# Routing each token tile inside the self-attention loop, with overflow blocks numbered as tiles open them

## The chip, the cores and the metric

The kernel runs on one core of one Trainium2 chip. The metric is the device time of one execution in microseconds (us). Three executions gave 1191.19 to 1192.11, with a median of 1192.05.

The core's engines run side by side: TensorE (PE, matrix products and transposes), VectorE (DVE), ScalarE (ACT), GpSimd (POOL) and SyncE (SP, which starts most transfers). Each works through its own list of instructions in order and waits for the others by semaphores.

## The reference

The program is a small network of two layers on `x` of 16 sequences x 64 tokens x 256 features: six residual sub-blocks, each behind a layer norm. What matters here is the third, the sub-block `L0_ffn`: an attention and then a mixture of 8 experts, of which each token uses two.

```python
h = _layernorm(x, ln1_g, ln1_b)
x = x + attention(h, Wq, Wk, Wv) @ Wo            # 16 heads of 16, within each sequence
m = _layernorm(x, ln2_g, ln2_b)
probs = jax.nn.softmax(m @ Wg, axis=-1)          # 8 experts
wts, idx = jax.lax.top_k(probs, 2)
wts = wts / jnp.sum(wts, axis=-1, keepdims=True)
h1 = jax.nn.gelu(einsum('td,edf->etf', m, W1) + b1[:, None, :])     # F = 1024
ye = einsum('etf,efd->etd', h1, W2) + b2[:, None, :]
moe_out = sum over the two chosen experts of wts * ye
return x + moe_out
```

Before it stands `L0_attn` (a latent attention with rotary parts, "mla" in the code), after it a cross attention, a causal attention ("attn") and a dense feed-forward part.

## The kernel before

The 1024 tokens are 8 tiles (`T`) of 128 rows; `x[:, t, :]` stays on chip. The stages run one after the other on every engine's list: `*_x0` (first cross attention), `*_self(span 0)`, `*_moe`, `*_x1`, `*_self(span 1)`, `*_ff`.

`*_self(span 0)` handles 16 items, the list `ITEMS`: mla of tiles 0, 1, 2, then in turn ffn (the attention of `L0_ffn`) of tile t-3 and mla of tile t, and at the end the ffn attention of tiles 5, 6, 7. So items 3, 5, 7, 9, 11, 13, 14, 15 are "ffn". The loop is software pipelined by hand: iteration n does the front of item n (transposed input `hT`, `q`/`k`/`v` or `rope`/`lat`/`qkc`, then the `scores`) and the back of item n-1 (`neg`, `exponents`, `pv`, `T`, `y`). The order on each engine is that of the calls in `pe_self`, `act_self`, `dve_self`, `pool_self`. Everything that TensorE hands over goes through four PSUM banks used in turn: the list `SA_FILLS` is the order of the fills, and `Ring.wait_free` makes a fill wait until the fill four places earlier has been read. The scores use four other banks.

On VectorE iteration n has: `k` or `rotate`, (`residual(n-2)` where item n is mla), `norm(n+1)`, `attend(n-1)`, `maximum(n)` (three instructions: a reduction of 128x1024 and two small ones that make `neg`), then `residual(n-1)`, which also starts the statistics of the next norm. GpSimd turns statistics into a factor (`row_rstd`) and adds `u` to `x` (`add_u`).

`*_moe` begins when the last item is finished. All 8 tiles are normed (`row_apply` "moe", 8 instructions, L372), transposed by TensorE (L1761) and scaled by ScalarE (`mT`, L1847), multiplied with `Wg` (`router`, L1752). VectorE takes the two largest of 8 (L1921, L1923), makes `pick` (which expert is first, which second choice) and `picked`. TensorE turns `picked` into ranks by matmuls with a triangle `before` and with `ones` (L1769 to L1774). Rows of expert e go to slots 256e to 256e+255 of the DRAM array `moe_in`; rows of rank 256 and more go to overflow blocks behind the eight first ones (NB = 15 blocks of 256 rows in all, the loop always computes all 15). VectorE works out the slots (L1939 to L1964), GpSimd then scatters each tile's rows twice, by an indirect transfer each (L2066, 16 in all). SP waits for the 16, loads blocks of `moe_in` (`xg<-moe_in`), and TensorE starts on block 0: `rows_T(0)` (L1794), `hidden(0)` (L1809).

Beside this stand: `gate`, the weights of the two experts per token, which TensorE transposes (L1779) and multiplies with `b2` (L1784) before `rows_T(0)` in its list; VectorE adds the result to `x` (L2008) before its part of `rows_T(0)` (L2015, L2017). Expert weights are split into a high and a low part: `expert_upper` on ScalarE, `expert_lower` on VectorE (L1737), `expert_lower_pool` on GpSimd (L1742).

## Time and profile before

| | |
|---|---|
| median of 3 runs | 1192.05 us |
| the profiled execution: its time, its span | 1194.0 us, 1192.0 us |
| busy in the span: PE, DVE, ACT, POOL | 1048.1, 617.5, 476.6, 240.5 us |
| `*_self(span 0)`: first `hT` to the last `residual` | 376.0 to 562.95 us |
| from there to `hidden(0)` | 562.95 to 615.94 us |

The profile was taken of one execution; its span runs from the first instruction to the last. "Idle before" in a row is the time in which the engine had nothing to do before this instruction, with what released it. PEclk is the share of TensorE's full clock (2.4 GHz) that was granted in a stretch: 0.50 is the lower of its two levels, 1.2 GHz, all the time.

### The profile page before, as it was taken

To read this page: it belongs to the slowest core of one execution; us is meant where nothing else is said; L and a number is where in the kernel's file an instruction comes from. 1 tells how busy PE (TensorE), PEld (TensorE's weight loads), DVE (VectorE), ACT (ScalarE), POOL (GpSimd) and SP (SyncE) were. 2 spreads that over 40 slices of the span, in tenths; PEclk is the share of its full clock that TensorE was granted. 3 is DMA by queue.
4 is the path that set the end of the run, shared out by engine and by line. 5 is a ranking of instruction groups with operands and counts; after the bars stand their busy time and mean duration, and the time that the engine had idled before them with its cause. 6 is when DMAs were issued, how large, how long until landed. Compare 5 with 4: busy or idle time off the path is not lost.

```text
span 1192.0 us, 27308 instructions
## 1 busy us (share of the span) xinstructions
PE 1048.1 (88%) x11708; PEld 902.8 (76%) x11708; DVE 617.5 (52%) x1205; ACT 476.6 (40%) x868; POOL 240.5 (20%) x381
## 2 busy tenths in 40 slices
PE   3999999999996899997539999986999988997998
PEld 3778888888875777775539999975878766775787
DVE  3745445454223444443628999965565632344342
ACT  1423333332322544553326677742434331443332
POOL 2211211211111121212343444423201000010000
PEclk9999999999998798997579999997999986997999
DMA  9200000000003400000065666622110002000000
GB/s 306 73 19 19 15 5 19 1 1 1 1 1 129 182 2 2 2 2 2 23 206 180 235 206 230 221 72 79 37 38 19 2 2 63 2 2 1 1 18 18
DMA packets 55670, 72.77 MB, mean 61 GB/s; under 512 B 8504, under 2 KB 48896, under 8 KB 54912
## 3 DMA queue, kind: packets, MB, share of 16 engines
q1 hardware_dynamic: 54016, 66.85, 16.8%
q0 software_dynamic: 1536, 4.20, 1.1%
...
q14 instruction: 25, 0.20, 0.1%
...
## 4 chain that ended last, share of the span: by engine, by line
PE 73%; DVE 12%; ACT 6%; issue 4%; POOL 3%; DMA 1%; DVEq 0%; SPq 0%; ACTq 0%; POOLq 0%
PE ps L1809 6%; PE ps L1827 6%; PE ps L527 5%; PE ps L2141 5%; PE ps L512 5%; PE ps L1384 4%; PE ps L991 3%; PE ps L1312 3%; PE ps L545 3%; PE ps L565 3%; PE ps L466 3%; PE ps L496 2%; PE ps L1346 2%; PE ps L928 2%; ACT sa_pT L1500 2%
## 5 line engine op out<-in xcount | busy, mean ns | idle before, releaser
L350 POOL TENSOR_TENSOR rn_tmp<-rn_cur,eps 128x1 f32<-128x1 f32 x48 | 13.4, 280 | 505.0 <-DVE rn_cur L344 505.0
L641 ACT ACTIVATE x0pT<-ps 128x512 f32<-128x512 f32 x64 | 38.3, 598 | 120.6 <-PE ps L527 120.6
L1809 PE MATMUL ps<-moe_xT_hi,ew_1hi 128*128 128x256 f32 x240 | 69.0, 287 | 2.3 <-DVE moe_xT_lo L2017 2.3
L1827 PE MATMUL ps<-ew_2hi,eh_hi 128*128 128x256 f32 x240 | 69.3, 289 | 1.1 <-DVE eh_lo L2025 1.1
L1809 PE MATMUL ps<-moe_xT_lo,ew_1hi 128*128 128x256 f32 x240 | 68.5, 286 | 0.0
L1809 PE MATMUL ps<-moe_xT_hi,ew_1lo 128*128 128x256 f32 x240 | 68.4, 285 | 0.0
L1827 PE MATMUL ps<-ew_2hi,eh_lo 128*128 128x256 f32 x240 | 67.4, 281 | 0.0
L1827 PE MATMUL ps<-ew_2lo,eh_hi 128*128 128x256 f32 x240 | 67.4, 281 | 0.0
L2023 DVE CAST eh_hi<-eh 128x512 fp32r<-128x512 f32 x60 | 58.8, 980 | 13.1 <-ACT eh L1878 13.0
L2025 DVE TENSOR_TENSOR eh_lo<-eh,eh_hi 128x512 fp32r<-128x512 f32 x60 | 60.2, 1003 | 2.1
L805 POOL TENSOR_SCALAR x0pT<-x0pT 128x512 f32<-128x512 f32 x64 | 39.3, 614 | 105.2 <-ACT x0pT L641 103.4
L1384 PEld LDWEIGHTS ps<-sa_v,sa_pT 64*64 64x64 f32 x1536 | 48.5, 139 | 15.3 <-ACT sa_pT L1500 15.3
L2141 PE MATMUL ps<-f,ffw 128*128 128x512 f32 x256 | 59.3, 391 | 0.3 <-DVE f L2212 0.3
L730 DVE COPY x0v<-ps 128x512 f32<-128x512 f32 x32 | 22.1, 691 | 68.9 <-PE ps L512 68.9
L1384 PE MATMUL ps<-sa_v,sa_pT 64*64 64x18 f32 x1536 | 50.9, 211 | 6.1 <-ACT sa_pT L1500 3.5
L2141 PEld LDWEIGHTS ps<-f,ffw 128*128 128x128 f32 x256 | 47.7, 188 | 10.9 <-DVE f L2212 1.1
L512 PE MATMUL ps<-x0wv_hi,x0cT_hi 128*128 128x512 f32 x128 | 53.3, 416 | 0.0
L724 DVE TENSOR_TENSOR x0A_lo<-ps,x0A_hi 128x512 fp32r<-128x512 f32 x64 | 40.5, 684 | 23.1 <-ACT x0A_hi L632 23.1
L527 PE MATMUL ps<-x0A_hi,x0cT_hi 128*128 128x512 f32 x128 | 51.3, 401 | 0.0
L512 PE MATMUL ps<-x0wv_hi,x0cT_lo 128*128 128x512 f32 x128 | 50.8, 397 | 0.0
L1742 POOL TENSOR_TENSOR ew_1lo<-ew,ew_1hi 128x1024 fp32r<-128x1024 f32 x15 | 39.1, 2608 | 57.5 <-ACT ew_1hi L1732 57.5
L512 PE MATMUL ps<-x0wv_lo,x0cT_hi 128*128 128x512 f32 x128 | 50.7, 396 | 0.0
...
## 6 DMA issues: line engine op xcount, KB each, us to landing
...
```

Of the source, the lines that this page charges most:

```text
L512: last = nc.tensor.matmul(dst, m[:, k, tok * P:tok * P + P], w[:, k, half * 512:half * 512 + 512], start=(k == 0 and n == 0), stop=(k == K ...
L527: last = nc.tensor.matmul(ps[:, S_BANK[u % 2], :], w[:, k, keys], m[:, k, b, pg, :, :, :].rearrange("p a j n -> p (a j n)"), start=(k == 0 ...
L641: nc.scalar.activation(g.pT[:, u, :], ps[:, S_BANK[u % 2], :], ACT.Exp, scale=64.0 ** -0.5).then_inc(C0.exp, 1)
L724: nc.vector.tensor_tensor(g.A_lo[:, kc, :, pg, par, :, :].rearrange("p b j n -> p j b n"), bank_of(t, f"A{gr}{par}").rearrange("p (j b n) ...
L805: nc.gpsimd.tensor_scalar(g.pT[:, u, :], g.pT[:, u, :], high, low, ALU.min, ALU.max).then_inc(C0.clip, 1)
L1384: last = nc.tensor.matmul(RS.bank(n, "pv")[rows_b, hd * XVW:hd * XVW + XVW], g.pT[rows_b, r, at_p:at_p + N], g.v[n % 2][rows_b, hd, :], st ...
L1742: nc.gpsimd.tensor_tensor(lo, w, hi.bitcast(F32), ALU.subtract).then_inc(MO.w_lo_pool, 1)
L1809: last = nc.tensor.matmul(ps[:, n % 3, j * BT:j * BT + BT], w[b % 2][:, i, f * P:f * P + P], v[b % 2][:, i, :], start=(i == 0 and m == 0), ...
L1827: last = nc.tensor.matmul(ps[:, O_BANK[b % 2] + c, 0:D], v[n % 3][:, j * BT + c * P:j * BT + c * P + P], w[b % 2][:, f, :], start=(f == 0 ...
L2023: nc.vector.tensor_copy(eh_hi[n % 3][:, :], eh[n % 3][:, :]).then_inc(MO.hi, 1)
L2025: nc.vector.tensor_tensor(eh_lo[n % 3][:, :], eh[n % 3][:, :], eh_hi[n % 3][:, :].bitcast(F32), ALU.subtract).then_inc(MO.split, 1)
L2141: last = nc.tensor.matmul(ps[:, 2 + f % 4, :], w[:, k, f * P:f * P + P], src[part][:, k, :], start=(k == 0 and part == 0), stop=(k == ks - ...
```

## The change

The work of the routing moves from `*_moe` into `*_self(span 0)`, one tile at a time:

- Behind the last fill of iteration n, where item n-2 is ffn (and item n is not mla), TensorE transposes the normed tile (`fill_mT(n-2)`). VectorE norms that tile (`moe_norm(n-2)`) behind `maximum(n)`. ScalarE scales it (`mT`).
- An iteration later, where item n-3 is ffn, TensorE does `fill_router(n-3)` and `fill_rank(n-3)`, VectorE `route_top`, `route_rank` and `route_slot`, GpSimd the two scatters of the tile. These three kinds of fills are new entries of `SA_FILLS`, so they take banks of the ring.
- Five tiles are routed inside the loop (at n = 6, 8, 10, 12, 14). Those of items 13, 14 and 15 are routed in a written-out end behind the loop, in which the back of item 15 stands too.
- A tile's slots must be known before later tiles are counted. So an expert's rows 256 and up no longer go to blocks numbered by expert, but to the next free block when a tile makes the count pass the end of the current one. `block_end`, `block_off`, `next_block`, `end_slot` carry this from tile to tile; the owner of each overflow block is found at the end from `opened`.
- The splits of expert 0 move one iteration forward on ScalarE and VectorE, and from `pool_moe` into iterations 14 and 15 on GpSimd.

```diff
         SA_FILLS = []
         for _lo, _hi in SPANS:
...
                 if is_mla(_n):
-                    SA_FILLS += [(_n, "rope")] + [(_n - 1, "neg")] * (_n > _lo) + [(_n, "lat")] + [(_n - 2, "y")] * late_y(_n - 2)
-                    SA_FILLS += [(_n - 1, "pv")] * (_n > _lo) + [(_n, "qkc"), (_n, "v")] + [(_n - 1, "T")] * (_n > _lo) + [(_n + 1, "hT")]
+                    SA_FILLS += [(_n, "rope")] + [(_n - 1, "neg")] * _bk + [(_n, "lat")] + [(_n - 3, "router")] * _rt + [(_n - 2, "y")] * late_y(_n - 2)
+                    SA_FILLS += [(_n - 1, "pv")] * _bk + [(_n, "qkc"), (_n, "v")] + [(_n - 1, "T")] * _bk + [(_n - 3, "rank")] * _rt + [(_n + 1, "hT")]
...
         def pe_self(pe, span):
...
+            if span == 0:
+                fill_neg(hi - 1)
+                fill_router(hi - 3)
+                exponents(hi - 1)
+                fill_mT(hi - 2)
+                fill_pv(hi - 1)
+                fill_rank(hi - 3)
+                fill_router(hi - 2)
+                fill_T(hi - 1)
+                fill_y(hi - 1)
+                fill_rank(hi - 2)
+                fill_mT(hi - 1)
+                fill_router(hi - 1)
+                fill_rank(hi - 1)
...
         def dve_self(dve, span):
...
+            def moe_norm(n):
+                t = ITEMS[n][1]
+                dve.wait_ge(SA.x_done, t + 1)
+                row_apply(dve, t, u[:, t, :], [u[:, t, :]], "moe")
...
+                route = span == 0 and is_ffn(n - 3)
                 if is_mla(n):
                     rotate(n)
                 elif front:
                     k(n)
+                if is_mla(n) and route:
+                    route_top(dve, n - 3)
                 if late_y(n - 2):
                     residual(n - 2)
...
                 if is_mla(n):
                     v(n)
+                    if route:
+                        route_rank(dve, n - 3)
                 if front:
                     maximum(n)
+                if route and not is_mla(n):
+                    route_rank(dve, n - 3)
+                if span == 0 and is_ffn(n - 2):
+                    moe_norm(n - 2)
+                if route:
+                    route_slot(dve, n - 3)
                 if back and not late_y(n - 1):
                     residual(n - 1)
-                if span == 0 and n > hi - 2:
-                    expert_lower(dve, 0, 2 * (n - hi + 1))
+                if span == 0 and n >= hi - 2:
+                    expert_lower(dve, 0, 2 * (n - hi + 2))
...
+            if span == 0:
+                route_top(dve, hi - 3)
+                moe_norm(hi - 2)
+                attend(hi - 1)
+                route_rank(dve, hi - 3)
+                route_slot(dve, hi - 3)
+                route_top(dve, hi - 2)
+                residual(hi - 1)
+                route_rank(dve, hi - 2)
+                moe_norm(hi - 1)
+                route_slot(dve, hi - 2)
+                route_top(dve, hi - 1)
+                route_rank(dve, hi - 1)
+                route_slot(dve, hi - 1)
...
         def pool_self(pool, span):
...
+                if span == 0 and is_ffn(n - 3):
+                    scatter(n - 3)
+                if span == 0 and n in (hi - 2, hi - 1):
+                    expert_lower_pool(pool, 0, 2 * (n - hi + 2) + 1)
...
+        def route_slot(dve, n):
+            t = ITEMS[n][1]
+            dve.wait_ge(MO.route, ROUTE[t, "opens"])
+            nc.vector.tensor_tensor(oless[:, :, :], less[:, :, :], each(opens[:, t:t + 1, :], (E, E)), ALU.mult).then_inc(MO.route, 1)
...
+            nc.vector.tensor_copy(slot[:, 2 * t:2 * t + 2], slotf[:, t, :]).then_inc(MO.slot, 1)
...
+            nc.vector.tensor_tensor(opened[:, t, :], block_id[:, :], opens[:, t, :], ALU.mult).then_inc(MO.route, 1)
...
+            nc.vector.tensor_tensor(end_slot[:, :], block_off[:, :], block_end[:, :], ALU.add).then_inc(MO.route, 1)
```

**Place 1: TensorE, from iteration 5 into iteration 6.** L1392/L1416 are the transposes `T`, L1281/L1305 `hT`, L1295/L1319 `rope`, L1353/L1377 `neg`, L1400/L1424 `y` (line of before / of the change). Before:

```order
L1392 MATMUL ps<-cst,sa_att 128x128 x2
L1281 MATMUL ps<-cst,h 128x128 x2
L1295 MATMUL ps<-sa_hT,w_mla 128x128 x8
L1353 MATMUL ps<-identb,sa_neg 128x128
L1287 MATMUL ps<-sa_hT,w_mla 128x128 x2
```

The change, the same place:

```order
L1416 MATMUL ps<-cst,sa_att 128x128 x2
L1305 MATMUL ps<-cst,h 128x128 x2
L1431 MATMUL ps<-cst,u 128x128 x2
L1319 MATMUL ps<-sa_hT,w_mla 128x128 x8
L1377 MATMUL ps<-identb,sa_neg 128x128
L1311 MATMUL ps<-sa_hT,w_mla 128x128 x2
```

The two transposes of the normed tile (L1431, `fill_mT`) now stand between `hT` and `rope`.

**Place 2: VectorE, from the end of iteration 6 into iteration 7.** L1578/L1668 is the last of `maximum`, L1596/L1686 with `u` the start of `residual(5)`, L1568/L1658 the copy `k(7)`. Before:

```order
L1578 SCALAR_TENSOR_TENSOR sa_neg<-sa_max,sa_neg 128x4x4
L1596 TENSOR_TENSOR u<-ps,u 128x256
L341 BN_STATS rn_st<-u 128x6
L344 BN_AGGR rn_cur<-rn_st 128x2
L1568 COPY sa_kT_133<-ps 128x256
```

The change, the last of the 16 instructions of `route_slot(3)` and what follows:

```order
L1927 TENSOR_TENSOR block_off<-block_off,moved_n 128x8
L1928 SCALAR_TENSOR_TENSOR block_end<-opens,block_end 128x8
L1930 TENSOR_SCALAR next_block<-next_block,opens_n 128x8
L1932 TENSOR_TENSOR end_slot<-block_off,block_end 128x8
L1686 TENSOR_TENSOR u<-ps,u 128x256
L359 BN_STATS rn_st<-u 128x6
L362 BN_AGGR rn_cur<-rn_st 128x2
L1658 COPY sa_kT_147<-ps 128x256
```

All 16 stand between `maximum(6)` and `residual(5)`, and so ahead of `k(7)`.

**Place 3: TensorE, the end of span 0.** Before, behind `scores(15)`:

```order
L1392 MATMUL ps<-cst,sa_att 128x128 x2
L1400 MATMUL ps<-w_sq_65,sa_attT 128x256 x2
L1353 MATMUL ps<-identb,sa_neg 128x128
L1366 MATMUL ps<-sa_negT,pick_neg 128x128 x4
L1370 MATMUL ps<-sa_qbd_131,sa_kT_133 64x128 x8
```

The change, from the same transposes `T(14)` to `pv(15)` (L1408):

```order
L1416 MATMUL ps<-cst,sa_att 128x128 x2
L1431 MATMUL ps<-cst,u 128x128 x2
L1424 MATMUL ps<-w_sq_65,sa_attT 128x256 x2
L1377 MATMUL ps<-identb,sa_neg 128x128
L1438 MATMUL ps<-wg,sa_mT 128x8 x2
L1390 MATMUL ps<-sa_negT,pick_neg 128x128 x4
L1394 MATMUL ps<-sa_qbd_145,sa_kT_147 64x128 x8
L1390 MATMUL ps<-sa_negT,pick_neg 128x128 x4
L1394 MATMUL ps<-sa_qbd_145,sa_kT_147 64x128 x8
L1431 MATMUL ps<-cst,u 128x128 x2
L1408 MATMUL ps<-sa_v_149,sa_pT 64x18 x32
```

`mT(13)`, `router(13)` and `mT(14)` have come in ahead of `y(14)`, of the exponents of item 15 and of its `pv`.

## Rows read from the trace of the kernel before

**Rows 1.** The page: busy time of each engine and share of the span

```profile
PE 1048.1 (88%) x11708; PEld 902.8 (76%) x11708; DVE 617.5 (52%) x1205; ACT 476.6 (40%) x868; POOL 240.5 (20%) x381
```

**Rows 2.** Windows (stretch, busy us per engine, PEclk, DMA share, GB/s), the scatter

```profile
583.00:612.00 29.00, 8.29 (x40) 6.50 (x40) 11.38 (x41) 4.33 (x6) 19.77 (x18) 0.62 0.25 84
```

**Rows 3.** Windows, two pairs of iterations, cut where `rope` starts on PE

```profile
446.09:469.32 23.23, 21.84 (x344) 18.12 (x344) 9.81 (x28) 10.64 (x23) 4.71 (x14) 0.87 0.01 3
...
491.40:512.08 20.68, 19.29 (x345) 15.93 (x345) 9.82 (x28) 10.64 (x23) 4.71 (x14) 1.00 0.01 2
```

**Rows 4.** Chain that ended last (start us, us, what), from the last residual on

```profile
562.95 0.43 DVE u L1596
...
586.58 0.18 DVE slot L1964
...
587.63 1.22 POOL moe_in L2066
...
607.32 2.40 DMA moe_in<-u,slot
...
614.73 0.44 DVE moe_xT_hi L2015
...
615.94 4.13 PE ps L1809 x21
```

**Rows 5.** Timeline around a `rope` (start us, us, engine, line, operation, idle before)

```profile
491.40 2.05 PE L1295 MATMUL ps<-sa_hT,w_mla 128*128 128x128 f32 x16 [0.77 <-ACT sa_hT L1462]
491.58 0.17 DVE L1578 SCALAR_TENSOR_TENSOR sa_neg<-sa_max,sa_neg 128x16 bf16<-128x16 f32 x1
```

**Rows 6.** Timeline of an ffn iteration: `residual`, `v`, `add_u`, `pv`

```profile
482.86 0.42 DVE L1596 TENSOR_TENSOR u<-ps,u 128x256 f32<-128x256 f32 x1
...
485.21 0.72 POOL L1652 TENSOR_TENSOR x_res<-x_res,u 128x256 f32<-128x256 f32 x1
...
485.70 1.13 PE L1322 MATMUL ps<-w_sq,sa_hT 128*128 128x256 f32 x4
...
486.95 2.04 PE L1384 MATMUL ps<-sa_v,sa_pT 64*64 64x18 f32 x64
```

**Rows 7.** Timeline, small VectorE instructions of the routing

```profile
584.31 0.21 DVE L1943 TENSOR_TENSOR slot_e<-ps,e 128x64 f32<-128x64 f32 x1
584.44 0.21 DVE L1945 TENSOR_TENSOR mless<-less,more 128x64 f32<-128x64 f32 x1
...
585.15 0.17 DVE L1951 TENSOR_TENSOR at_over<-at_over,e 128x8 f32<-128x8 f32 x1
585.35 0.22 DVE L1953 SCALAR_TENSOR_TENSOR over_e<-ps,at_over 128x64 f32<-128x64 f32 x1
```

**Rows 8.** Timeline, end of `qkc` on ACT and start of `scores` on PE

```profile
499.75 0.36 ACT L1475 ACTIVATE sa_kT<-ps,col 128x128 f32<-128x128 f32 x1
...
500.26 0.60 PE L1340 MATMUL ps<-causalb,identb 128*128 128x256 bf16 x4 [0.38 <-ACT sa_kT L1475]
```

**Rows 9.** Timeline, `y(14)` and `pv(15)` on PE

```profile
552.36 1.13 PE L1400 MATMUL ps<-w_sq,sa_attT 128*128 128x256 f32 x4 [0.47 <-ACT sa_attT L1509]
...
556.31 2.56 PE L1384 MATMUL ps<-sa_v,sa_pT 64*64 64x18 f32 x64 [1.18 <-ACT sa_pT L1500]
```

**Rows 10.** Line L372, one of its forms (ns min/median/max, first and last start)

```profile
L372 DVE TENSOR_SCALAR u<-u,rn_mean,rn_rs x8: 401/402/2428, 566.9 to 573.2; 128x256 f32<-128x256 f32 x8
```

**Rows 11.** Timeline, GpSimd at work beside VectorE norms, in two stages

```profile
566.84 2.34 POOL L1742 TENSOR_TENSOR ew_1lo<-ew,ew_1hi 128x1024 fp32r<-128x1024 f32 x1
...
817.95 1.04 POOL L2083 DMA_INDIRECT yg<-moe_out,slot  x1 [0.19 <-issue]
...
818.16 0.38 DVE L372 TENSOR_SCALAR h<-x_res,rn_mean,rn_rs 128x256 f32<-128x256 f32 x1
```

**Rows 12.** Timeline, the products with `b2` and their addition to `x`

```profile
591.13 5.69 PE L1784 MATMUL ps<-b,gate_T 128*128 128x256 f32 x16 [1.18 <-ACT gate_T L1856]
...
596.86 2.48 DVE L2008 TENSOR_TENSOR x_res<-ps,x_res 128x512 f32<-128x512 f32 x4 [3.46 <-PE ps L1784]
```

355 lines of the change are left out of this document (201 added, 154 removed).

## The prediction, made before the changed kernel was run

> **What bounds the kernel now.** I read the page first: PE is busy for 88% of the span, DVE for 52%, POOL for 20% [rows 1]. So almost everywhere time is TensorE's, and the holes in its work are what a change can win. The windows show the largest hole: from 583 to 612 us PE is busy for 8.29 of 29 us, while POOL is busy for 19.77 [rows 2]. The chain of waits says what fills it. The last residual of the self-attention starts at 562.95, the slots are cast at 586.58, the scatters begin at 587.63, the last lands 2.40 us after 607.32, and `hidden(0)`, the first product of the experts, starts at 615.94 [rows 4]. That is 52.99 us, in which the attention has nothing left to do. The loop ahead of it is the opposite: a pair of iterations (mla and ffn) takes 20.68 us where PE has its full clock and is busy for 19.29 of it, DVE only for 9.82 [rows 3]. So the change takes work out of a hole and puts it into a loop in which PE has 1.4 us to spare and VectorE much, but in which PE waits for VectorE at fixed places.
>
> **Behind the loop: what is won.** Let R be the start of `residual(15)` and S the cast of the last tile's slots.
>
> *R to S.* Before: 586.58 - 562.95 = 23.63 us. After, only tile 7's own chain is left. From `residual` to the end of `add_u` it takes 485.21 + 0.72 - 482.86 = 3.07 us in the loop [rows 6]. Then `moe_norm` (0.40, [rows 10]), two transposes, `mT` and the router: some 2.7 us, my estimate from the length of such a step before. VectorE meanwhile has `route_slot(14)`, 16 instructions. Dependent small ones start 0.20 us apart, independent ones 0.13 [rows 7]; with nine dependent at 0.2 to 0.25 and seven mostly free ones that makes 3.0 us, and it covers the transposes and the router. Then `route_top` 1.5 us (six instructions, one of two parts), the ranks on PE 0.5, `route_rank` 0.5, and eight more instructions to the cast, 1.8. Together 3.07 + 0.40 + 3.0 + 1.5 + 0.5 + 0.5 + 1.8, with waits in between 10.9 us. Won: 12.7.
>
> *S to `hidden(0)`.* Before: 615.94 - 586.58 = 29.36 us, since 16 scatters lie 1.31 us apart (607.32 - 587.63 over 15) [rows 4]. After, two follow S; their data would be on chip at about S + 8. But another chain then ends later, the one of `gate` and `b2`, which stands ahead of `rows_T(0)` in PE's list and is hidden by the scatters now. The products with `b2` started 591.13 - 586.58 = 4.55 us after S [rows 4, 12]. After, seven instructions of bookkeeping (1.05), the difference and exponential that were done early before (0.45), and ScalarE's four splits of expert 1 that now fall behind it (0.45) go in front: 6.5. Products and additions to `x` take 596.86 + 2.48 - 591.13 = 8.21 [rows 12], the split of `moe_xT` 615.94 - 614.73 = 1.21 [rows 4]. Sum 15.9, won 29.36 - 15.9 = 13.4. All 16 scatters and the transfers of SP behind them (it waits for the 16 as before) are off the path: ten go out in the loop, six here.
>
> Together 26.1 us are won.
>
> **The end of the loop: R gets later.** In the list of PE `mT(13)` now stands ahead of `y(14)`, and `mT(14)` ahead of `pv(15)`. `mT(13)` waits for `moe_norm(13)`, which VectorE starts only behind `maximum(15)`: `y(14)`, at 552.36 before [rows 9], goes to about 554.0. ScalarE then has `mT(13)` and a split before `neg`, so the exponents of item 15 come 2.2 us later. `mT(14)` needs `add_u(14)`, which is 3.07 us after `residual(14)` at 555.1, itself late, plus the statistics of a GpSimd that is slowed there: 559.1, norm and transposes to 560.3. So `pv(15)` starts at 560.3 for 556.31 [rows 9]. Behind `attend(15)` VectorE has `route_rank(13)`, `route_slot(13)`, `route_top(14)`, 5 us, against 3.3 us that PE and ScalarE need to `y(15)`: 1.65 more. So R is 5.65 us later. On top, the norm of item 14 starts just when GpSimd begins a split: beside such a one (2.34 us [rows 11]) a norm took 2.428 for 0.40 us [rows 10], so 2.0 more. I take 7.65; the ends are 5.65 and, if `moe_norm(13)` is caught too, 8.75.
>
> **In the loop.** Three waits are added; each is read from one pair.
>
> *`mT` before `rope` (n = 5, 7, 9, 11).* `rope` starts at 491.40, held by ScalarE's `hT`; the last instruction of `maximum` starts at 491.58 [rows 5], the norm behind it ends at 492.08, transposes 0.35: `rope` at 492.45. 1.05 us, four times 4.2. At n = 13 it is `y(12)` that waits in the same way, 1.4.
>
> *`route_slot` ahead of `residual` and `k`.* The residual at 482.86 moves by 3.0 us and frees its bank at 486.3; `v`, four fills on, started at 485.70 [rows 6] and has to wait 0.6. `pv` follows by the same, since there `k` too is read only at 487.5 for 486.95 [rows 6]. Four times 0.6 is 2.4. What waits behind `route_slot` in VectorE's list (the `u` statistics, the norm for item n+2) has slack.
>
> *A longer ring.* With `rank` in it `hT(n+1)` stands four fills behind `qkc`, so it waits until ScalarE has read that at 500.11; then transposes, then `scores`, which started at 500.26 [rows 8]. With 0.2 for the router that is 0.5, four times 2.0.
>
> *n = 14 and 15.* Router 0.3; `expert_lower` has moved ahead of `k(15)`, so `pv(14)` waits 0.95. Sum 1.25. GpSimd's scatters, 2 x 1.31 us, stand ahead of `add_bias` and the next `row_rstd`, which are not due for several us: nothing.
>
> Loop: 4.2 + 1.4 + 2.4 + 2.0 + 1.25 = 11.25. The first cross attention and everything from `hidden(0)` on stay: the same 15 blocks, in other numbers.
>
> **Sum.** -26.1 + 7.65 + 11.25 = -7.2 us. The profiled execution took 1194.0 us and would take 1186.8; it lay 1.95 above the median of the runs, so the median comes to 1184.85, say 1185.
>
> **A rule weighed.** Ten scatters now run on GpSimd beside VectorE's norms. A norm beside a GpSimd transfer took 0.38 us, its usual time, and the transfer 1.04 us [rows 11]. I count nothing. The Trainium skill (SBUF — State Buffer, "Who interferes with whom") calls the port pair that both share an exclusive lock for a whole instruction, which speaks against this change; by it each norm under a scatter could wait for the scatter. What the row shows is not that, and the sum would be 5 x 1.3 us worse if it were.
>
> **The rivals.**
> 1. *The norms are caught under the scatters after all.* In the pair GpSimd finishes `add_u` at about 488.9, so its scatters lie at 489.0 to 491.6 and the bias addition behind them beside `moe_norm`. Against it the row above; for it the 2.428 us beside an ordinary GpSimd instruction. Five norms by 1.3 us, and with them PE: 6.5 more, 1191.5: no change.
> 2. *TensorE's clock falls more often.* This ends on the other side. In the pair from 446.09 the granted clock was 0.87 and it took 23.23 us, 2.55 more than the one at 1.00 [rows 3]. The change puts a second hole of about a us into each pair, at `mT`. With fewer than three pairs more at the lower clock it is still a gain; with four more it is 1185 + 10.2 = 1195. Against it: PE had 0.77 us of idle there already [rows 5], in a pair that kept its clock; one of the two pairs shown didn't. The Trainium skill (TensorE: Matmul & The Clock Gate, "A second HAM failure mode") tells of a kernel whose short idles between groups made the clock go up and down; the pair at 0.87 may be such a case.
> 3. *The insertions hide better.* If the waits in the loop cost no more than PE's added work, about 0.85 us a tile (transposes, router, ranks at full clock, an estimate), 8 x 0.85 = 6.8, and the norms are not caught (5.65), then -26.1 + 5.65 + 6.8 = -13.65: 1178.4.
> 4. *The gate chain is not the last.* If the scatters' chain ends later than S + 15.9, say by slower single transfers, the gain shrinks by what it exceeds; from the rows it has 6 us of slack. Within the range.
>
> **How the numbers follow.** Forecast 0.55 (its own range 1181 to 1189), rival 1 0.12, rival 2 0.16, rival 3 0.17. About 0.2%, 2.4 us, is what a measurement of this kernel can tell. Faster by more: the forecast nearly whole (0.52), rival 3 (0.17), a little of rival 2 with one or two falls (0.02): 0.71. No change: 0.03 + 0.12 + 0.02 less a part of rival 1 that is slower: 0.15. Slower: 0.14. The range takes in rival 3 and rival 1, and leaves out the worse half of rival 2: 1177 to 1193.
>
> **What would show it.** The pairs between two `rope`s grow from 20.68 to about 22.8 us. In the rows of `rope` the releaser is then the transposes of `u`, not `hT`. `hidden(0)` starts near 609. S lies 11 us behind R, and `hidden(0)` 16 behind S, released by the additions of `b2` (L2008) and not by `xg`. The prediction is wrong if pairs grow by more than 3.5 us (a fourth wait, or the clock), or if R is over 10 us later than the loop alone makes it.

## The result: slower by 0.34%

The changed kernel took 1195.73 us (median of 8 executions, 1194.20 to 1198.55), the kernel before 1191.57 us (8 executions, 1191.14 to 1195.69). The ratio is 1.0034 with a 95% interval of 1.0020 to 1.0048. Run again later (12 executions against 17 of before) it was 1.0039, interval 1.0017 to 1.0062. The forecast was 1185.0 with a range of 1177 to 1193, faster with a chance of 0.71: wrong in sign. Its two largest terms were right, and the loss came from the loop, which it had priced at 11.25 us.

The page of the changed kernel, busy time of each engine, to be read against [rows 1]: TensorE is busy for 10 us more, VectorE for 26.

```profile
PE 1058.3 (88%) x11715; PEld 911.5 (76%) x11715; DVE 643.6 (54%) x1374; ACT 477.7 (40%) x868; POOL 241.9 (20%) x381
```

Windows of both kernels, cut at the same four places: from the `rope` of item 4 to the start of `maximum(15)`; to R, the start of `residual(15)`; to S, the last cast of slots; to `hidden(0)`. Before:

```profile
425.41:551.59 126.18, 119.42 (x2047) 98.94 (x2048) 56.11 (x156) 61.69 (x131) 26.69 (x82) 0.95 0.01 2
551.59:562.95 11.36, 8.02 (x117) 5.40 (x116) 4.40 (x9) 3.95 (x6) 3.76 (x7) 0.76 0.01 1
562.95:586.58 23.63, 11.01 (x64) 9.89 (x64) 15.50 (x56) 10.43 (x21) 7.14 (x6) 0.50 0.00 1
586.58:615.94 29.36, 8.78 (x29) 6.64 (x29) 10.07 (x29) 3.33 (x5) 20.71 (x18) 0.62 0.34 115
```

The changed kernel:

```profile
423.92:575.27 151.35, 137.87 (x2091) 115.53 (x2092) 75.90 (x291) 67.40 (x142) 40.53 (x93) 0.85 0.03 11
575.27:595.82 20.55, 13.47 (x132) 9.87 (x132) 12.70 (x44) 4.63 (x9) 5.65 (x6) 0.50 0.00 1
595.82:605.60 9.78, 2.19 (x12) 1.53 (x12) 6.71 (x42) 0.81 (x2) 5.50 (x8) 0.50 0.16 55
605.60:622.66 17.06, 8.96 (x28) 7.03 (x29) 16.25 (x37) 7.27 (x10) 6.97 (x4) 0.60 0.64 208
```

| stretch | before | after | difference | forecast |
|---|---|---|---|---|
| start to `rope` of item 4 | 425.41 | 423.92 | -1.49 | 0 |
| loop | 126.18 | 151.35 | **+25.17** | +11.25 |
| end of the loop to R | 11.36 | 20.55 | +9.19 | +7.65 |
| R to S | 23.63 | 9.78 | -13.85 | -12.7 |
| S to `hidden(0)` | 29.36 | 17.06 | -12.30 | -13.4 |
| `hidden(0)` to the end | 576.06 | 574.14 | -1.92 | 0 |
| sum | 1192.0 | 1196.8 | +4.80 | -7.2 |

The loop lost nearly all that was won elsewhere. In its window PE's busy time grew by 18 us for 44 more instructions, and PEclk fell from 0.95 to 0.85: much of that is the same products at the lower clock. TensorE's idle time in it grew by 6.7 us (151.35 - 137.87 against 126.18 - 119.42).

What the loop looks like inside. First the hole that the forecast expected, in the timeline of TensorE around the `rope` of item 6:

```profile
447.95 0.69 PE L1431 MATMUL ps<-cst,u 128*128 128x128 f32 x2 [1.50 <-DVE u L390]
448.43 3.62 PE L1319 MATMUL ps<-sa_hT,w_mla 128*128 128x128 f32 x16
```

`mT` waits 1.50 us for the norm behind `maximum`. A `rope` took 2.05 us in [rows 5]; this one takes 3.62, which is the 1.2 GHz level for nearly all of it. All five ropes from item 4 on are like that (3.78, 3.62, 3.36, 3.62, 3.29 us); before, two of five were (3.78 and 3.45).

The first of the five slow ropes is not the change's. The routing's first instruction on TensorE is the `mT` at 447.95, and the clock is down around the `rope` of item 4 (423.92), long before it. Three windows of the changed kernel, the last column but two is PEclk:

```profile
421.92:423.92 2.00, 1.26 (x29) 0.92 (x25) 1.61 (x3) 0.90 (x3) 0.00 (x0) 0.77 0.00 0
423.92:429.92 6.00, 6.00 (x53) 5.15 (x61) 1.93 (x8) 0.28 (x1) 0.00 (x0) 0.51 0.01 3
429.92:445.92 16.00, 15.38 (x296) 12.69 (x297) 6.64 (x18) 9.48 (x19) 4.72 (x14) 1.00 0.01 3
```

Of the 17 profiles in which that stretch has the same work (all but the one with `rope` filled), this rope was slow in five: the changed kernel, the changed kernel again, both kernels with plain transfers, and scatters beside `rope`. Where it was fast, the pair that it opens was 2.6 us shorter (21.89 for 24.51 us). So 2.6 us of the 25.17 are chance, and loops can be compared only with that said. The profiles of the changed kernel are also of two of its longer executions (1198.49 and 1203.38 us, for medians of 1195.73 and 1199.07).

Then something the forecast did not have. Timeline of GpSimd, TensorE and VectorE in the iteration of item 9, where the scatters of a tile are issued (L1784), `pv` has just ended, the scores (L1370) run, and VectorE wants to begin with the reciprocal (L1675) and the maximum (L1662):

```profile
494.29 1.05 POOL L1784 DMA_INDIRECT moe_in<-u,slot  x1 [0.17 <-issue]
494.82 1.23 PE L1370 MATMUL ps<-sa_kT,sa_qbd 32*128 32x64 f32 x28
495.65 0.97 POOL L1784 DMA_INDIRECT moe_in<-u,slot  x1 [0.30 <-issue]
496.34 0.45 PE L1370 MATMUL ps<-sa_kT,sa_qbd 32*128 32x64 f32 x4 [0.29 <-issue]
496.38 0.26 DVE L1675 RECIPROCAL sa_rinv<-ps 128x16 f32<-128x16 f32 x1 [3.35 <-PE ps L1408]
...
497.38 1.23 DVE L1662 TENSOR_REDUCE sa_max<-ps 128x16 f32<-128x1024 f32 x1 [0.28 <-PE ps L1370]
```

`pv` ended at 494.89, and the reciprocal that waits only for it starts at 496.38, 1.5 us late. TensorE itself stops after 28 of its 32 products and goes on at 496.34. The scores, 1.12 us wherever in this loop no scatter is near, take 1.97 here. It isn't the clock: the profile grants 1.00 from 494.30 to 497.40.

Behind the loop, the chain from S to `hidden(0)` (start us, us, what), to be read against [rows 4] and [rows 12]:

```profile
605.60 0.17 DVE slot L1920
...
608.07 0.23 DVE gate L2100
...
609.09 2.71 DVE moe_of_expert L2108
...
616.89 1.13 DVE ew_1lo L1953
618.02 1.14 DVE ew_2lo L1953
619.15 2.40 DVE x_res L2128 x4
621.55 0.34 DVE moe_xT_hi L2135
...
622.66 1.43 PE ps L1993 x5
```

It is VectorE's list without a break. The additions of `b2` (L2128) stand in it as forecast, but what they waited for was VectorE itself, not the products.

### The profile page after: what moved, and what is told of

Same layout as the page of the kernel before. It is cut to its first block, busy times and chain, and to the rows that moved or that the text cites. A ratio compares the mean times of both kernels' runs of the same rounds, so it can differ in the third digit from the quotient of the medians.

```text
span 1196.8 us, 27530 instructions
## 1 busy us (share of the span) xinstructions
PE 1058.3 (88%) x11715; PEld 911.5 (76%) x11715; DVE 643.6 (54%) x1374; ACT 477.7 (40%) x868; POOL 241.9 (20%) x381
## 4 chain that ended last, share of the span: by engine, by line
PE 73%; DVE 16%; ACT 5%; issue 3%; POOL 2%; DMA 1%; DVEq 0%; SPq 0%; ACTq 0%; POOLq 0%
PE ps L1993 7%; PE ps L2011 7%; PE ps L545 6%; PE ps L530 5%; PE ps L2253 5%; PE ps L1408 4%; PE ps L1009 3%; PE ps L563 3%; PE ps L1370 3%; PE ps L484 3%; PE ps L583 2%; PE ps L1336 2%; PE ps L514 2%; PE ps L946 2%; PE ps L1319 2%
## 5 line engine op out<-in xcount | busy, mean ns | idle before, releaser
L368 POOL TENSOR_TENSOR rn_tmp<-rn_cur,eps 128x1 f32<-128x1 f32 x48 | 13.4, 279 | 516.3 <-DVE rn_cur L362 516.3
L1408 PEld LDWEIGHTS ps<-sa_v,sa_pT 64*64 64x64 f32 x1536 | 48.6, 138 | 13.7 <-ACT sa_pT L1576 12.7
L2253 PEld LDWEIGHTS ps<-f,ffw 128*128 128x128 f32 x256 | 47.8, 188 | 10.9 <-DVE f L2324 1.1
L1408 PE MATMUL ps<-sa_v,sa_pT 64*64 64x18 f32 x1536 | 51.0, 211 | 5.1 <-ACT sa_pT L1576 2.4
L545 PE MATMUL ps<-x0A_lo,x0cT_hi 128*128 128x512 f32 x128 | 50.5, 395 | 0.0
```

Of the source, the lines that this page charges most:

```text
L545: last = nc.tensor.matmul(ps[:, S_BANK[u % 2], :], w[:, k, keys], m[:, k, b, pg, :, :, :].rearrange("p a j n -> p (a j n)"), start=(k == 0 ...
L1408: last = nc.tensor.matmul(RS.bank(n, "pv")[rows_b, hd * XVW:hd * XVW + XVW], g.pT[rows_b, r, at_p:at_p + N], g.v[n % 2][rows_b, hd, :], st ...
L2253: last = nc.tensor.matmul(ps[:, 2 + f % 4, :], w[:, k, f * P:f * P + P], src[part][:, k, :], start=(k == 0 and part == 0), stop=(k == ks - ...
```

## The experiments

All are edits of the changed kernel. "Loop" is the first window above in each kernel's own profiled execution, one for each kernel; the ratio is to the kernel before, timed on the same chip.

| kernel | median us (runs) | ratio, 95% interval | loop us, PEclk |
|---|---|---|---|
| changed, again | 1199.07 (12) | 1.0039, 1.0017 to 1.0062 | 151.35, 0.85 (+) |
| all scatters behind the loop | 1195.58 (10) | 0.9999, 0.9979 to 1.0018 | 139.34, 0.90 |
| plain transfers by GpSimd | 1189.18 (10) | 0.9970, 0.9953 to 0.9987 | 143.23, 0.87 (+) |
| plain transfers by SP | 1189.45 (10) | 0.9946, 0.9920 to 0.9972 | 143.21, 0.87 (+) |
| one scatter a tile in the loop | 1188.80 (1) | - | 139.97, 0.90 |
| scatters of narrow rows | 1197.51 (1) | - | 148.01, 0.87 |
| `mT` later | 1187.75 (7) | 0.9934, 0.9909 to 0.9958 | 141.19, 0.90 |
| hole at `mT` filled | 1188.92 (9) | 0.9958, 0.9934 to 0.9982 | 142.22, 0.92 |
| slots later | 1191.88 (10) | 0.9976, 0.9954 to 0.9999 | 146.21, 0.88 |
| `mT` and slots later, scatters behind | 1191.34 (10) | 0.9966, 0.9941 to 0.9990 | 136.63, 0.88 |
| three moves | 1185.23 (10) | 0.9921, 0.9893 to 0.9948 | 147.11, 0.86 |
| scatters beside `rope` | 1185.58 (8) | 0.9908, 0.9874 to 0.9942 | 133.39, 0.92 (+) |
| the same, new tail | 1182.03 (4) | 0.9891, 0.9840 to 0.9942 | 136.67, 0.88 |
| the same, new VectorE list | 1184.00 (4) | 0.9893, 0.9837 to 0.9950 | 136.68, 0.88 |
| tail and list | 1181.38 (6) | 0.9877, 0.9833 to 0.9921 | 136.68, 0.88 |
| tail and list, `rope` filled | 1176.97 (6) | 0.9846, 0.9817 to 0.9875 | 131.77, 0.95 |

(+) marks a slow `rope` of item 4 in the profile, about 2.6 us that have nothing to do with the edit. Of the 15 executions of the kernel before beside the kernels from "scatters beside `rope`" to "tail and list" one took 3413 us, the other 14 1187 to 1200.

### The scatters

**Behind the loop.** Five scatter pairs leave GpSimd's loop, and all 16 stand behind it.

```diff
-                if span == 0 and is_ffn(n - 3):
-                    scatter(n - 3)
...
-                scatter(hi - 2)
-                scatter(hi - 1)
+                for n in range(lo, hi):
+                    if is_ffn(n):
+                        scatter(n)
```

> The changed kernel, with all 16 scatters issued behind the loop again (GpSimd alone is changed). In the changed kernel the scores of the ffn items take 2.45 us instead of 1.05 in the iterations in which GpSimd issues its scatters; about 1.4 us five times. Theory 'scatters': their transfers or GpSimd's issues hold TensorE up there; then those five scores go back to 1.1 us, the loop from the reference rope at 424 us to the end of scores(15) falls from 151.35 to about 144 us, and 16 scatters at 1.31 us behind the last slots put hidden(0) about 29 us behind S instead of 17: in sum 5 us slower than the changed kernel, about 1201 us. Theory 'clock' (the scores are long since TensorE runs at its lower level there): the loop stays within 1 us of 151.35, and the whole is 12 us slower, about 1208 us.

The scores are back at 1.12 to 1.18 us (one took 1.43), and the loop is 12.0 us shorter. 2.6 of that is the first pair, which has no scatter in either kernel and ran at 0.95 here and 0.85 there, so 9.4 belong to the rest. `hidden(0)` lies 22.58 us behind S: +5.5, less than the 12 expected, since six of the sixteen had been started before S. The time of the whole is that of before, 1195.58 us for the 1201 expected.

**What about a scatter is it?** Plain transfers of the same 128 KB, to fixed rows, by GpSimd and then by SP (the experts then get other tokens). In the second, `scatter` keeps its waits and signals SP, whose lines are these:

```diff
-                    nc.gpsimd.indirect_dma_start(moe_in, bass.IndirectOffsetOnAxis(slot[:, 2 * t + i:2 * t + i + 1], 0), u[:, t, :], None).then_inc(MO.spread, 16)
+                    nc.gpsimd.dma_start(moe_in[(2 * t + i) * P:(2 * t + i + 1) * P, :], u[:, t, :]).then_inc(MO.spread, 16)
```

```diff
+                pool.sem_inc(MO.go, 1)
...
+            for t in range(T):
+                sp.wait_ge(MO.go, t + 1)
+                for i in range(2):
+                    sp.dma_start(moe_in[(2 * t + i) * P:(2 * t + i + 1) * P, :], u[:, t, :]).then_inc(MO.spread, 16)
```

> The changed kernel; in place of each scatter by index GpSimd issues a plain transfer of the same tile, same size, to fixed rows of moe_in, at the same place in its list (the rows are not routed: the experts get other tokens, all else is computed). Now in the loop the reciprocal behind pv starts 2.0 to 2.1 us after the first scatter is issued, though pv ended 0.6 us after it, and the scores take 1.9 to 2.5 us. Theory 'the index form' (what GpSimd does to make a transfer by index holds the others up): both go back to what they are without scatters (reciprocal at once, scores 1.12 us), loop about 140 us. Rival 'the bytes' (the 128 rows of 1 KB that are moved hold them up): they stay as they are, loop 151 us or what the clock makes of it. Rival 'any issue by GpSimd': the same as the bytes here, told apart by the next kernel.

> As the kernel with plain transfers, but issued by SP on a signal from GpSimd, so that GpSimd issues nothing in the loop (rows again not routed). Theory 'any issue by GpSimd': scores 1.12 us and the reciprocal at once behind pv, loop about 140 us. Rival 'the bytes': scores 1.9 to 2.5 us as with scatters, for the same 256 KB a tile are moved at the same time.

Timeline of the kernel with plain transfers by GpSimd, in the iteration of item 11:

```profile
516.80 1.96 PE L1408 MATMUL ps<-sa_v,sa_pT 64*64 64x18 f32 x61
...
517.94 1.15 POOL L1784 DMA_DIRECT2D moe_in<-u  x2
...
518.69 1.12 PE L1370 MATMUL ps<-sa_kT,sa_qbd 32*128 32x64 f32 x32
518.80 0.26 DVE L1675 RECIPROCAL sa_rinv<-ps 128x16 f32<-128x16 f32 x1 [1.91 <-PE ps L1408]
```

The reciprocal starts 0.04 us behind `pv`, the scores take 1.12. Both kernels have loops of 143.2 us, with the same five slow ropes and the same slow first pair (24.64 and 24.66 us) as the changed kernel. So with as many slow ropes the form by index costs 151.35 - 143.22 = **8.1 us**; neither the bytes nor that GpSimd issues them does. Not all of it is the delay itself: the granted clock is 0.85 in the one loop and 0.87 in the other, about 45 and 37 us at the lower level (twice what PEclk lacks to 1, times the length). By the price found below (2.66 us for the 6.7 us at the lower level in a pair of 24.01 us at 0.86, 0.4 per us) that is some 3 of the 8.1, an estimate.

**Narrow rows, and one of two.** The rows carry 128 bytes instead of 1 KB; or the second scatter of each tile goes behind the loop.

```diff
-                    nc.gpsimd.indirect_dma_start(moe_in, bass.IndirectOffsetOnAxis(slot[:, 2 * t + i:2 * t + i + 1], 0), u[:, t, :], None).then_inc(MO.spread, 16)
+                    nc.gpsimd.indirect_dma_start(moe_in.rearrange('r (a b) -> (r a) b', b=32), bass.IndirectOffsetOnAxis(slot[:, 2 * t + i:2 * t + i + 1], 0), u[:, t, 0:32], None).then_inc(MO.spread, 16)
```

```diff
-                    scatter(n - 3)
+                    scatter(n - 3, (0,))
...
+                for n in range(lo, hi):
+                    if is_ffn(n):
+                        scatter(n, (1,) if n < hi - 2 else (0, 1))
```

> The changed kernel with the scatters by index moving 128 bytes a row instead of 1 KB (the first 32 features; the experts read other data, all else is computed). Theory 'the index form': the same 128 rows by index, so scores 1.9 to 2.5 us and the reciprocal 2 us behind the scatter's start, as now, though an eighth of the bytes moves. Rival 'bytes and index together': less than half of the delay.

> The changed kernel with only the first of each tile's two scatters in the loop, the second behind it. What holds up the hand-over from TensorE ends 2.03 to 2.10 us after the first scatter's start where one instruction is waited for, and 1.4 to 1.5 us after the second's start in two other places. Theory 'each scatter by itself': the reciprocal still starts 2.0 us behind the scatter, but the last scatter of the loop holds up only once. Rival 'the two together' (the second stands behind the first's descriptors): the reciprocal at once, scores 1.12 us.

Timeline of the kernel with narrow rows, in the iteration of item 9:

```profile
489.45 1.05 POOL L1784 DMA_INDIRECT moe_in<-u,slot  x1 [0.17 <-issue]
...
490.80 0.97 POOL L1784 DMA_INDIRECT moe_in<-u,slot  x1 [0.30 <-issue]
491.50 0.45 PE L1370 MATMUL ps<-sa_kT,sa_qbd 32*128 32x64 f32 x4 [0.29 <-issue]
...
491.54 0.26 DVE L1675 RECIPROCAL sa_rinv<-ps 128x16 f32<-128x16 f32 x1 [3.37 <-issue]
```

The same place in the kernel with one scatter:

```profile
489.91 2.04 PE L1408 MATMUL ps<-sa_v,sa_pT 64*64 64x18 f32 x64 [0.20 <-DVE sa_kT L1658]
...
491.35 1.06 POOL L1784 DMA_INDIRECT moe_in<-u,slot  x1 [0.17 <-issue]
...
491.88 1.30 PE L1370 MATMUL ps<-sa_kT,sa_qbd 32*128 32x64 f32 x32
...
492.73 0.26 DVE L1675 RECIPROCAL sa_rinv<-ps 128x16 f32<-128x16 f32 x1 [2.64 <-PE ps L1408]
```

With an eighth of the bytes the reciprocal still starts 2.09 us behind the first scatter. The loop, 148.01, is 3.3 us under the changed kernel's, and 2.6 of that is the fast `rope` of item 4. With a single scatter it starts 1.38 us behind it, 0.78 late, and the scores take 1.30; the loop, 139.97, is only 0.6 us over the one without any. Neither theory for this pair was right as put: a lone scatter does hold up the hand-over, but most of the cost comes with the second, right behind the first.

### The hole at `mT`

**Later.** TensorE's `fill_mT` and ScalarE's `mT` move behind `neg` of the next iteration (behind the loop `router(13)` then follows the exponents).

```diff
@@ pe_self, both kinds of iteration
                     if back:
                         fill_neg(n - 1)
+                    if route:
+                        fill_mT(n - 3)
...
-                    if span == 0 and is_ffn(n - 2):
-                        fill_mT(n - 2)
@@ act_self
+                if span == 0 and is_ffn(n - 3):
+                    mT(n - 3)
```

> The changed kernel, with the transposes of the normed tile (mT) and ScalarE's scaling moved from ahead of rope into the next iteration, behind the neg transpose, where the norm is long done. Theory 'hole and clock' (the wait of mT for the norm behind maximum makes a hole of 1.1 to 1.85 us ahead of each rope, and rope then runs at the lower clock, 3.3 to 3.8 us for 2.05): rope goes back to about 2.1 us, the first pair from 24.5 to about 21 us, the routed ones from 25.7 to about 23, in sum -10 us or more in the loop, about 1185 us. Rival 'waits only' (the hole as I priced it, 1.05 us four times and 1.4 once, the clock does what it wants): -5 us, about 1190 us. Rival 'the hole moves' (another wait ends last, the chain through maximum, neg and exps): within 1 us of the changed kernel.

**Filled.** The hole stays, with 12 useless products in it.

```diff
+                RS.wait_free(pe, n, "mT")
+                if n < 13:
+                    for k in range(12):
+                        nc.tensor.matmul(RS.bank(n, "mT")[:, 0:D], identb[:, :], causalb[:, :].rearrange("p (o n) -> p o n", o=1).broadcast_to((P, 4, N)),
+                                         start=True, stop=True, skip_group_check=True)
                 pe.wait_ge(rn_done, ROW_APPLIED["moe", n])
-                RS.wait_free(pe, n, "mT")
```

> The changed kernel, with 12 useless products of 128x128 by 256 columns put ahead of TensorE's wait for the norm in mT of items 3 to 11; nothing reads them. They take 1.3 us at full clock, about as long as the hole of 1.1 to 1.85 us that the wait leaves. Theory 'hole and clock': the idle itself makes the clock fall, so with work in it rope runs at full clock (2.1 us for 3.3 to 3.8), the granted clock of the pairs goes from 0.83 to 0.91 up to 0.95 or more, and each pair is 1.5 to 2.5 us shorter although work was added: about 1187 us. Rival 'waits only': the pairs keep their length within 0.5 us, about 1196 us. Rival 'load lowers the clock': more work, lower clock, longer pairs, 1198 us or more.

Windows from one `rope` to the next, first two pairs of the changed kernel:

```profile
423.92:448.43 24.51, 22.38 (x346) 18.61 (x347) 10.47 (x30) 10.65 (x23) 4.72 (x14) 0.85 0.01 2
448.43:474.65 26.22, 23.50 (x353) 19.54 (x353) 13.54 (x54) 11.72 (x25) 6.96 (x16) 0.83 0.04 13
```

and of the one with the hole filled:

```profile
424.02:446.92 22.90, 22.27 (x359) 18.42 (x359) 10.46 (x30) 10.65 (x23) 4.72 (x14) 0.93 0.01 3
446.92:470.99 24.07, 23.20 (x366) 19.16 (x365) 13.52 (x54) 11.72 (x25) 6.95 (x16) 0.93 0.04 14
```

The second pair has 12 more products and is 2.2 us shorter. The first can't be read like that: its `rope` of item 4, ahead of any hole, was fast here and slow there. Against a first pair with the hole and a fast rope (21.89 us) the filled one, 22.90, is 1.0 us longer. The loop is 9.1 us shorter with 60 more products, of which 2.6 are that rope: **6.5** for the filling. The ropes of items 6 to 12 take 2.00, 1.95, 1.95 and 2.83 us, for 3.62, 3.36, 3.62 and 3.29. The filling doesn't keep the clock from falling: it is at 0.50 in the two us from 444.02, as the useless products begin, but back at 1.00 in those from 448.02, where the changed kernel runs its `rope` at 0.50. The products are about as long as the hole, so its own length is still paid: the 6.5 us are what it costs by the clock of the work behind it. The timed executions agree: the mean granted clock of the whole was 0.930 to 0.938 in the nine of this kernel, 0.918 to 0.931 in the 20 of the changed one. This is what the Trainium skill (TensorE: Matmul & The Clock Gate, "A second HAM failure mode: psum-queue depth-cycling") tells of another kernel, micro-idles that make the clock go up and down; this case agrees, with 6.5 us.

`mT` later shortens the loop by 10.2 us, 7.5 without the rope of item 4: between "waits only" and "hole and clock". Its first pair is that of before to the hundredth (20.68 us, 0.97), 1.2 us under the 21.89 with the hole. But the expected return of the ropes did not come: those of items 6 to 12 take 3.78, 3.78, 3.68 and 3.49 us, and the pairs (25.12, 24.86, 24.35) keep the scatters too. In the eight profiles with an open hole at `mT` all 32 ropes of items 6 to 12 were slow (3.10 to 3.62 us); in the seven with `mT` later, 25 of 28; in that of before, two of four. So taking the hole away gives back its own length; the idle of 0.56 to 0.77 us that is left ahead of `rope` may be what holds the clock down then; filling that one is tried below.

### The slots

`route_slot` goes behind `norm(n + 1)` of the next iteration, the scatters follow it there.

```diff
@@ dve_self
-                if route:
-                    route_slot(dve, n - 3)
+                if span == 0 and is_ffn(n - 4):
+                    route_slot(dve, n - 4)
@@ pool_self
-                if span == 0 and is_ffn(n - 3):
-                    scatter(n - 3)
+                if span == 0 and is_ffn(n - 4) and n < hi:
+                    scatter(n - 4)
```

> The changed kernel, with route_slot (16 small instructions of VectorE, 2.5 us) moved from ahead of the residual into the next iteration, behind k and the norm for item n+2; the two scatters follow one iteration later. My price for its old place was 0.6 us in four pairs, 2.4 us. If that holds: 1193.4 us, and the waits of v and pv for VectorE go. If a wait that shortens also keeps TensorE's clock up, -5 us or more. If the hole at mT decides everything, no change within 1 us.

The loop is 5.1 us shorter, of which 2.6 are again the clock of the first pair. The other 2.5 look like the 2.4 forecast for the old place, but the scatters moved with the slots and their cost with them, so this run doesn't show the price of the slots alone. The scatters show where else they bite: they now start beside the scores of an mla item, which keep their 1.12 us, but the maximum behind them starts 1.44 us after the second scatter's start (508.79), 2.1 us late.

### Together, and the place beside `rope`

**Both moves, scatters behind** (the diffs of these three together):

> The same two moves of mT and route_slot, but all scatters behind the loop. The loop is then free of scatters: 131 us, and each pair 21 to 22 us. hidden(0) lies 22.6 us behind S as with the scatters behind the loop alone, 5.5 more than now. Sum about 1182 us. If the loop stays over 137 us, a cause that I haven't named is in it: added work of TensorE and VectorE, or the longer ring.

**Three moves**: `mT` and slots later, and in GpSimd's list a wait for `hT(n + 1)` ahead of the scatters:

> The changed kernel with mT moved behind neg of the next iteration, route_slot moved behind k and the norm of the next one, and the scatters held until hT of the next mla item is filled, so that they run beside rope, where TensorE hands nothing over for 2 us. If the three places are what costs the loop its 25 us (mT's hole, the slots ahead of the residual, the scatters beside pv and scores), the loop goes from 151 to 133 us, and the whole to about 1180 us. If they give the stall only another place, 1188 us as with mT alone.

The second did not do what its text says: `row_rstd` stands ahead of the scatters in GpSimd's list and waits for a residual in the middle of the next iteration, so they came 13 us later and again held up the maximum. Its loop stayed at 147.1 us. It took 1185.23 us for the 1180 expected. The first reached 136.63, without a scatter, for 131 expected, and 1191.34 us for 1182; its pairs of 24.01 us run at 0.86, so what its loop lacks to the 131 is the clock, with neither hole at `mT` nor scatter in it.

**Beside `rope`**: the scatters ahead of `row_rstd`.

```diff
                     add_bias(n + 1)
+                if span == 0 and is_ffn(n - 4) and n < hi:
+                    if is_mla(n + 1):
+                        RS.wait_filled(pool, n + 1, "hT")
+                    scatter(n - 4)
                 if n > lo:
```

> As the kernel with three moves, but the scatters now stand ahead of row_rstd in GpSimd's list, so that they really run beside rope (there they ran 13 us later, beside the scores of an mla item, and the maximum behind these came 1.5 us behind the second scatter's start). If a scatter only delays what TensorE hands to VectorE, it costs nothing beside rope: loop 135 us or less, no maximum or reciprocal with a remote releaser for tiles 0 to 2, about 1181 us. If it delays TensorE itself wherever it is, rope gets longer by 1 to 1.5 us and the loop stays above 140 us.

Timeline, scatters beside the `rope` of item 8:

```profile
468.69 1.22 POOL L1788 DMA_INDIRECT moe_in<-u,slot  x1 [4.33 <-PE ps L1305]
469.15 2.05 PE L1319 MATMUL ps<-sa_hT,w_mla 128*128 128x128 f32 x16 [0.77 <-ACT sa_hT L1541]
470.22 0.97 POOL L1788 DMA_INDIRECT moe_in<-u,slot  x1 [0.30 <-issue]
471.24 1.13 DVE L1650 SCALAR_TENSOR_TENSOR rope<-ps,col,cst 128x128 f32<-128x128 f32 x4 [1.24 <-PE ps L1319]
```

`rope` keeps its 2.05 us, VectorE takes it over 0.04 us behind its end, and that pair lasts 21.35 us at a clock of 1.00. The loop, 133.39, is within the 135 expected, the whole 4.6 us over the 1181. The loops of the next three kernels, with the same code there, came to 136.68 with their pairs at 0.86, equal to the kernel without scatters: beside `rope` they are free. 21.35 against 24.01 is also the price of the clock in a pair: **2.66 us**.

But it needn't be `rope`. Of the five tiles only three have an mla item behind them; the fourth tile's scatters stand beside `pv` and the scores in these kernels too, at a place like the ones that were hit, and nothing waits. Timeline of the kernel with the new tail:

```profile
535.30 2.04 PE L1408 MATMUL ps<-sa_v,sa_pT 64*64 64x18 f32 x64
535.81 1.05 POOL L1788 DMA_INDIRECT moe_in<-u,slot  x1 [1.53 <-DVE slot L1927]
...
537.28 1.12 PE L1370 MATMUL ps<-sa_kT,sa_qbd 32*128 32x64 f32 x32
537.39 0.26 DVE L1679 RECIPROCAL sa_rinv<-ps 128x16 f32<-128x16 f32 x1 [1.17 <-PE ps L1408]
```

The second scatter starts at 537.17. The reciprocal starts 0.05 us behind `pv`, 1.58 behind the first scatter, and the scores keep their 1.12 us.

**Tail** (`pv(15)` ahead of `mT(14)`, `residual(15)` ahead of `route_top(14)`, and the fills to match) and **VectorE's list** (`rows_T(0)` ahead of the wait for the products with `b2` and the four additions; owners' biases and the splits of expert 1 behind `hidden(1)`), and both:

```diff
-                fill_mT(hi - 2)
                 fill_pv(hi - 1)
+                fill_mT(hi - 2)
```

```diff
             rows_T(0)
+            dve.wait_ge(MO.b2_ps, 1)
...
             hidden(1)
+            expert_lower(dve, 1, 0)
+            expert_lower(dve, 1, 2)
```

> The kernel with the scatters beside rope, and a new order behind the loop: pv(15) ahead of mT(14), residual(15) ahead of the top-two of item 14. My price of the tail was 7.65 us from these orders; measured 9.2. From the end of scores(15) to R the kernel with three moves needs 16.6 us. Theory 'orders': R comes 2.5 us earlier (14 us), S stays 9.8 to 10.5 us behind R, in sum -2 us, about 1179 us. Rival: S is set by the chain of bookkeeping and moves by less than 0.5 us.

> The kernel with the scatters beside rope, and in VectorE's list behind the last slots: the split of moe_xT ahead of the additions of b2; the owners' biases and the two splits of expert 1 behind hidden(0) and hidden(1). Now hidden(0) starts 17.05 us behind S, at the end of an unbroken list of VectorE. Theory 'VectorE's list was last': hidden(0) at S + 11 to 13 us, in sum -3 us or more, about 1178 us. Rival 'the scatters' own chain' (last scatter at S + 2, landing, load of xg, transposes): S + 15 or more, -1 us.

> The last three together: mT and slots moved, scatters beside rope, the new order behind the loop and the new list of VectorE. If the gains add: 1176 us, against 1191.6 of before and 1195.7 of the changed kernel. If the clock takes part of it back (pairs at 0.86 as with no scatters in the loop), 1182 us.

End of the loop to R: 19.50 us without, 14.74 with the new tail, S again 9.80 behind R: 4.8 us, more than expected. S to `hidden(0)`: 17.06 us to 14.82 with the new list, 2.2 us; what ends last then is the chain of the products with `b2` (5.91 us from 596.20). The tail gave more than expected, the list less, and with both the clock stayed at 0.86 in the pairs, the second case of that expectation. The medians, 1182.03 and 1184.00, lie above the 1179 and 1178 expected. In the timed medians the three can't be told apart from the kernel without them; the intervals overlap.

**`rope` filled.** Six useless products ahead of the wait for `hT`, in the kernel with tail and list.

```diff
+                RS.wait_free(pe, n, "rope")
+                if n > 3:
+                    for k in range(6):
+                        nc.tensor.matmul(RS.bank(n, "rope")[:, 0:D], identb[:, :], causalb[:, :].rearrange("p (o n) -> p o n", o=1).broadcast_to((P, 4, N)),
+                                         start=True, stop=True, skip_group_check=True)
                 RS.wait_emptied(pe, n, "hT")
-                RS.wait_free(pe, n, "rope")
```

> The kernel with all orders changed, and six useless products of 256 columns ahead of TensorE's wait for hT in rope of items 4 to 12 (0.64 us at full clock, where TensorE sits idle for 0.56 to 0.77 us). In its profile all four later ropes ran at the lower clock: pairs of 24.01 us at 0.86 where one at 1.00 takes 21.35. Theory 'idle ahead of rope makes the clock fall': ropes of 2.05 us, pairs of 21.5 to 22.5 us, in sum -6 to -10 us, 1173 to 1176 us. Rival: the clock falls for the load of the whole pair, and the filling adds up to 0.3 us a pair; 1182 us.

The window of the pair of item 8 in the kernel with tail and list:

```profile
469.71:493.72 24.01, 22.91 (x353) 19.19 (x354) 14.60 (x55) 11.55 (x25) 6.94 (x17) 0.86 0.04 13
```

and with `rope` filled:

```profile
468.40:489.76 21.36, 20.70 (x359) 17.28 (x359) 14.71 (x55) 11.52 (x25) 6.96 (x17) 1.00 0.04 15
```

The loop is 4.9 us shorter, less than the 6 to 10 expected: of the ropes of items 6 to 12 two are back at 2.05 us, the others take 2.80 and 2.39. It is the difference of one profile each. "Scatters beside `rope`", unfilled, had two fast ropes of these four by itself (2.05 and 1.83 us), and its loop of 133.39 has a slow `rope` of item 4: without that it would be 130.8. So the 4.9 us may be in part luck. The six executions had a mean clock of 0.935 to 0.942, the six unfilled ones 0.926 to 0.940. The whole, 1176.97 us, is the fastest here: 1.5% under before (0.9846, 0.9817 to 0.9875).

**The changed kernel again.**

> The changed kernel itself once more, because the runs of the kernel before spread over 1187 to 1200 us on the chips of the experiments, where they spread over 1191 to 1196 when the change was measured. If the loss of 0.34% is the change's: ratio 1.002 or more to before again. If it hung on how often TensorE's clock fell in the runs of that one chip, which five slow ropes of five in the changed kernel's profile against two of five before suggest (8 us), the ratio lies within 1.000 plus or minus 0.002.

1.0039, and a loop of 151.35 us to the hundredth. The loss is the change's, and the second profile has the slow `rope` of item 4 as well.

## Why the prediction was wrong

**Bound and gain (right).** The work did leave the hole behind the attention: R to S shrank by 13.85 (forecast 12.7), S to `hidden(0)` by 12.30 (13.4), 26.15 together for 26.1. S lies 9.8 us behind R for 10.9, `hidden(0)` 17.06 behind S for 15.9. Within the second, the path was the wrong one of two near-equal chains: "released by the additions of `b2`" it was, but what these waited for was VectorE's own list, which ended 2.2 us behind the products with `b2`, as the new list showed.

**End of the loop (right in kind, 1.5 us too small).** 9.19 for 7.65. The norm of item 14 was caught beside a GpSimd split as priced. In the chain of waits (start us, us, what; "issue" ahead of the norm L390 is where it was held):

```profile
583.90 2.03 issue
585.93 1.10 DVE u L390
...
587.08 0.69 PE ps L1431 x2
587.77 3.56 PE ps L1408 x64
591.36 0.27 DVE sa_rinv L1675
...
595.91 0.34 DVE u L1686
```

(The chain's pieces don't overlap, so R is 595.91 here and 595.82 in the timeline.) The excess stands in the same rows: `pv(15)` ran at 1.2 GHz, 3.56 us where [rows 9] have 2.56, and the norm took 1.10 on top of its wait.

**The loop (the step that failed).** 25.2 us for 11.25. An estimate of its parts from the rows above. The loop spends about 45 us at the lower clock for 13 before (0.15 and 0.05 of its length, doubled); at 0.4 us each the 32 more make 13 us. Of these 2.6 are the `rope` of item 4, chance, and 3 go with the scatters. The scatters' own delay is the other 5 of their 8.1. The remaining 7 are the waits and the added work that I had priced at 11.25. So the priced terms were too high by 4, and two things had no term:

- "GpSimd's scatters ... stand ahead of `add_bias` and the next `row_rstd`, which are not due for several us: nothing." They cost 8.1 us. The scatters were weighed only by what is queued behind them on GpSimd, and by whether they slow a VectorE norm. Neither happened, and rival 1 (norms caught under the scatters) is wrong: in the loop every norm took 0.41 us, behind it one beside a scatter took 0.45, and of three under scatters beside `rope` two took 0.41 and one 0.57. The rule of the Trainium skill on the port pair (SBUF — State Buffer, "Who interferes with whom") gave no cost under a scatter here, and it adds that TensorE never waits on anyone. It speaks of SBUF's ports. Whatever the path is here, the rows of the iteration of item 9 differ: TensorE stops in the middle of its scores while two scatters are issued. [rows 11] could not show that: the only transfer by index beside other work there stood beside a norm, with no product shown running.
- The clock as a term. It was rival 2, at 0.16, "with four more pairs 1195", and the sum took it as nothing. The argument against it, that one of two pairs shown had kept its clock with 0.77 us of idle, was one sample of a chance: with this same idle and unchanged work around it, the `rope` of item 4 was slow in five of 17 profiles, and with the change's hole ahead of it every `rope` from item 6 on was slow (32 of 32).

The scatters' 8.1 us alone would have turned the forecast's -7.2 us into +0.9. In full: -7.2, 13 for the clock, 5 for the scatters' own delay, less 4 for the priced waits, plus 1.5 of the tail and less 3.4 at start and end, give 4.9 for the 4.8 of the two spans.

**What stays open.** Why two transfers by index hold up TensorE's issue and its hand-over to VectorE. Shown is that they do in the changed kernel and its near relatives, five times in the loop, and that bytes, issuer and plain form do not. Not every transfer by index ahead of a hand-over does it: the fourth pair in the kernels with the scatters beside `rope` held up neither `pv` nor scores (535.81 above). Behind the loop VectorE's small instructions go on 0.2 us apart beside scatters, ScalarE takes the transposes of 599.41 over at 600.14, 0.04 us behind their end, and VectorE the router's products at once. What the spared places have that the others lack isn't shown. Whether the records' "issue" means that TensorE's sequencer stood still or that its completions were reported late can't be told from them. That the whole gains from filling `rope` beyond the loop's 4.9 us is not shown: the two kernels were timed at different times, and their intervals overlap.
